# Mamba block with a top-2 mixture of LoRA experts on one core: new orders of the side jobs between the scans

## The chip, the cores and the metric

The kernel runs on one core of a Trainium2 chip. The metric is the device time of one launch in microseconds (us); of several runs the median counts.

## What is computed

The input is `u` with 4 sequences of 2048 tokens of 256 numbers. The block is pre-norm, with two residual branches:

```
x = u + mamba(layernorm(u));  out = x + moe(layernorm(x))
mamba:  x, z = split(u @ W_in.T + b_in)                       # 512 and 512 columns
        dt, B, C = split(x @ W_x.T + b_x)                     # 16, 16, 16
        delta = softplus(dt @ W_dt.T + b_dt);  A = -exp(A_log)
        h[t] = h[t-1] * exp(delta[t] * A) + x[t] * delta[t] * B[t]     # 512 x 16 states
        y[t] = sum over states of h[t] * C[t];  y = (y + x * D) * silu(z);  return y @ W_out.T + b_out
moe:    w = softmax(x @ Wg.T + bg), kept for the best 2 of 4 experts
        h_e = relu(x @ Wi.T + (x @ A_e.T) @ B_e.T);  return sum_e w_e * (h_e @ Wo.T)
```

All of it is in fp32. The recurrence over time is the part that no engine but VectorE does here, as a scan instruction.

## The kernel before

The 4 x 2048 tokens are cut into 16 chunks of 512 tokens, one after the other (the four sequences take turns). With 16 states for each of 512 channels, a chunk has 64 scans of 128 partitions x 512 tokens. They are grouped into 16 steps `s` of four scans `j`; four steps share a block `m` of 128 channels. The program below is each engine's own list of instructions, with semaphores between the lists. No scheduler moves anything: each engine works strictly through its list.

For each step there is a fixed skeleton:

- ScalarE (ACT) makes `decay = exp(delta * A)` for each scan into four PSUM banks (L1203), and keeps the last state of each scan (L1217, `keep_state`): after scans 0 and 1 have been multiplied by C, and after scans 2 and 3. The first two decays of a step can be made only after the keep for scans 0 and 1 of the step before.
- GpSimd (POOL) makes the scans' inputs `dx * B` for the next step (L1470, `times_b`), and in twelve of the 16 steps multiplies the last two scans by C (L1482, `times_c`).
- VectorE (DVE) does the four scans (L1395) and the other products with C (L1382).
- TensorE (PE) sums over the states into `y_ps` (L998, `sum_states`), two steps behind the scans. The sums of a block may start only when DVE has read the block before (`gated`, L1287).

All other work of the block is cut into small side jobs. A job is a letter and a number, and the same name stands in the tables of each engine that has a part in it. `pre` jobs belong to the next chunk, `main` to this one, `post` to the chunk before and `late` to the one before that. The jobs that the text speaks of, with their lines on PE and ACT or DVE:

- O: normalise the input (ACT L1159 on `xin`), for which GpSimd makes the last factor (L692). A: transpose it (PE L908). B, E: products with W_in (PE L914; B read by ACT at L1066, E at L1126). C, D: products that give B, C and delta (PE L918, L921; ACT L1101 is the last reader of a D).
- V, W, Z: after E, three more ACT steps for the sigmoid (L1129, L1132, L1135). S `main`: DVE multiplies it into `silu` (L1282), which frees E's bank. Y `main`: DVE makes `gated` (L1287).
- F: product with W_out and the residual (PE L933 to L940, ACT L1071). P, R, Q: second layer norm (ACT L1080, L1147 to L1153, L1159 on `xr`). G: transpose its result (PE L908 on `xr`, copied by ACT L1163). H0: the router's product (PE L946), read by DVE at L1325; H1 to H9, M0, M1: DVE's choice of the two experts.
- J, S: the two halves of the experts' hidden layer (PE L962 to L966 and L885; ACT L1177, L1181). T: transpose them (PE L979; ACT copy L1186). K: product with Wo (PE L984), added by DVE at L1298.
- L, M: ACT's exp and log for the softplus (L1108, L1113); V and U on GpSimd: the DMA that adds to it (L1460) and the product `delta * x` (L1450).

The order of the jobs is written out in tables, one row for each step. A row of PE has two parts (before and after `sum_states`), a row of ACT or DVE four, one behind each scan or decay:

```python
for job in side("act", c, s, j, parts):
    job_act(*job, c, par)
```

`SIDE` holds for chunks 0 to 14 (with small changes `FIRST` and `SECOND` for the start), `LAST` for chunk 15, `END` for what remains after the last scan. Products go to three PSUM banks. `assign_banks` runs through PE's table and gives each job the bank that, by the tables, is free first, so a new order also gives new banks, and with them new waits of PE for the engine that reads a bank.

Of the kernel before, what the change touches and what calls it, by code (L numbers as in the profile page):

```python
# [54 lines left out]
    "F1 post, F2 post, A1 pre | E0 main, F3 post, B0 pre",
    " | T3 late",
    "J4 late, B1 pre | B2 pre, B3 pre, S4 late",
    "E1 main | ",
    "J5 late, C0 pre | ",
    "C1 pre, K1 late, D0 pre | S5 late",  # L60
# [2 lines left out]
    "J6 late, J7 late, S6 late | ",
    "K2 late, S7 late | T6 late, E3 main",
    "T7 late, I0 post | K3 late",
    "J0 post, D2 pre | D3 pre, S0 post, J1 post",
    "J2 post, S1 post | T0 post",
# [1491 lines left out]
```

## Time and profile before

| | us |
|---|---|
| three runs | 1881.43, 1888.95, 1902.90 |
| median of the three | 1888.95 |
| the profiled execution | 1869.98 |
| its span, first to last instruction | 1868.2 |
| busy: DVE / GpSimd / PE / ACT | 1765.0 / 1717.0 / 1641.5 / 1505.7 |
| mean granted TensorE clock, share of full | 0.95 |

The profiled execution is 1.0% faster than the median of the others, which differ by 1.1% among themselves. Stage times below are of the profiled execution and count from the start of its span. Chunk 0's first scan starts at 39.8, chunk 8's at 910.5, chunk 15's at 1674.7, and the last scan ends at 1786.1.

### The profile page before, as it was taken

The numbers are of one execution on the slowest core, as the hardware profiler recorded it, in microseconds if no ns is written. First come the engines' busy times: TensorE is split into PE (matmuls) and PEld (weight loads), VectorE is DVE, ScalarE is ACT, GpSimd is POOL, SyncE is SP. The second block draws the span as 40 slices with busy tenths as digits, with TensorE's granted clock in tenths as the row PEclk, the third lists the DMA queues.
The fourth block names the chain that finished last, engine by engine and source line by source line (L and its number), as shares of the span: only waits on it lengthen the run. The fifth ranks groups of instructions, "written<-read, shape, count | busy, mean of one in ns | idle before, by whom it ended". The sixth has DMA issues, their size and how long they took to land.

```text
span 1868.2 us, 26288 instructions
## 1 busy us (share of the span) xinstructions
PE 1641.5 (88%) x7052; PEld 834.3 (45%) x7052; DVE 1765.0 (94%) x2060; ACT 1505.7 (81%) x3113; POOL 1717.0 (92%) x649
## 2 busy tenths in 40 slices
PE   6646689998998999899899989989998998998999
PEld 3213244444444444444444444444444544444465
DVE  5999999999999999999999999999999999999941
ACT  4776789788888978888897888889788898977743
POOL 1999999999999999999999999999999999999810
PEclk9767889999999999999999999999999999999999
DMA  6565566656647565654756565575656657565100
GB/s 209 137 142 142 109 153 141 163 119 143 151 99 172 132 170 120 148 142 104 174 129 168 126 144 143 105 173 132 163 128 142 144 105 175 120 160 133 42 18 17
DMA packets 150070, 249.07 MB, mean 133 GB/s; under 512 B 22432, under 2 KB 47264, under 8 KB 149408
## 3 DMA queue, kind: packets, MB, share of 16 engines
q1 hardware_dynamic: 145456, 231.09, 51.2%
q0 software_dynamic: 4464, 16.25, 4.5%
q8 instruction: 61, 1.00, 0.2%
q14 instruction: 89, 0.73, 0.1%
HBM read 188.01 MB, written 42.99 MB: 124 GB/s over the span
## 4 chain that ended last, share of the span: by engine, by line
PE 38%; DVE 30%; issue 13%; ACT 8%; POOL 5%; DMA 2%; SPq 1%; DVEq 0%; ACTq 0%; POOLq 0%
DVE decay L1395 13%; DVE hs L1382 8%; PE bank L914 7%; DVE hs L1395 5%; PE y_ps L998 5%; PE bank L962 5%; PE bank L984 4%; PE bank L936 4%; POOL hs L1470 3%; PE bank L918 3%; ACT decay L1203 2%; POOL hs L1482 2%; PE y_ps L1002 2%; PE bank L908 1%; PE bank L979 1%
## 5 line engine op out<-in xcount | busy, mean ns | idle before, releaser
L1470 POOL TENSOR_TENSOR hs<-dx_rep,b_rep 128x2048 f32<-128x2048 f32 x255 | 1180.6, 4643 | 43.6 <-DVE hs L1411 39.7
L1395 DVE TENSOR_TENSOR_SCAN decay<-decay,state,hs 128x512 f32<-128x512 f32 x640 | 798.7, 1288 | 6.3 <-ACT decay L1203 5.2
L1203 ACT ACTIVATE decay<-dt_rep,a_sb 128x512 f32<-128x512 f32 x1024 | 696.2, 686 | 20.6 <-DVE dx_rep L1409 1.8
L1395 DVE TENSOR_TENSOR_SCAN hs<-decay,state,hs 128x512 f32<-128x512 f32 x384 | 491.5, 1280 | 3.9 <-ACT decay L1203 3.8
L1482 POOL TENSOR_TENSOR hs<-hs,c_rep 128x1024 f32<-128x1024 f32 x192 | 469.3, 2444 | 5.3 <-ACT state L1217 4.6
L1382 DVE TENSOR_TENSOR hs<-decay,c_rep 128x1024 f32<-128x1024 f32 x320 | 389.0, 1216 | 0.0
L998 PE MATMUL y_ps<-hs,nsum 128*32 128x512 f32 x2048 | 291.6, 643 | 61.4 <-POOL hs L1482 40.4
L962 PE MATMUL bank<-w_i_sb,x_t 128*128 128x512 f32 x488 | 259.9, 658 | 5.4 <-DVE silu L1282 5.1
L914 PE MATMUL bank<-xn_t,w_in_sb 128*128 128x512 f32 x512 | 249.8, 616 | 12.2 <-DVE silu L1282 4.3
L984 PE MATMUL bank<-w_o_sb,r_t 128*128 128x256 f32 x944 | 221.0, 388 | 10.3 <-ACT r L1181 6.2
L984 PEld LDWEIGHTS bank<-w_o_sb,r_t 128*128 128x128 f32 x944 | 177.6, 192 | 65.0 <-ACT r L1181 18.2
L1217 ACT COPY state<-decay 128x2 f32<-128x2 f32 x320 | 50.4, 157 | 159.8 <-DVE hs L1382 156.7
L914 PEld LDWEIGHTS bank<-xn_t,w_in_sb 128*128 128x128 f32 x512 | 91.7, 194 | 125.7 <-issue 98.3
L979 PE MATMUL bank<-ident,r 128*128 128x128 f32 x928 | 121.7, 277 | 17.2 <-DVE x L1298 14.3
L962 PEld LDWEIGHTS bank<-w_i_sb,x_t 128*128 128x128 f32 x488 | 89.1, 200 | 104.3 <-issue 86.3
L979 PEld LDWEIGHTS bank<-ident,r 128*128 128x128 f32 x928 | 101.8, 140 | 75.6 <-issue 42.7
L998 PEld LDWEIGHTS y_ps<-hs,nsum 128*32 128x32 f32 x2048 | 41.8, 110 | 172.5 <-issue 150.0
L936 PE MATMUL bank<-w_out_sb,gated 128*128 128x256 f32 x480 | 114.0, 380 | 0.1
L1181 ACT ACTIVATE r<-bank,wgt 128x512 f32<-128x512 f32 x122 | 82.3, 675 | 33.0 <-PE bank L885 33.0
L936 PEld LDWEIGHTS bank<-w_out_sb,gated 128*128 128x128 f32 x480 | 91.6, 191 | 13.2 <-DVE gated L1287 0.5
L885 PE MATMUL bank<-lora_st,low_t 64*128 64x512 f32 x122 | 61.0, 500 | 41.1 <-ACT r L1177 40.8
L1177 ACT ACTIVATE r<-bank,wgt 128x512 f32<-128x512 f32 x122 | 82.8, 678 | 15.5 <-PE bank L966 12.2
(182 smaller groups left out, 1853.8 us busy)
## 6 DMA issues: line engine op xcount, KB each, us to landing
dx_rep<-rep_scratch SPq DMA_DIRECT2D x252, 256.0 KB, 4.7
dt_rep<-rep_scratch SPq DMA_DIRECT2D x252, 256.0 KB, 7.6
b_rep<-bc_scratch SPq DMA_DIRECT2D x256, 64.0 KB, 4.0
c_rep<-bc_scratch SPq DMA_DIRECT2D x256, 64.0 KB, 2.4
rep_scratch<-z_dt SPq DMA_DIRECT2D x64, 256.0 KB, 2.6
rep_scratch<-e_dt SPq DMA_DIRECT2D x64, 256.0 KB, 2.8
e_dt<-z_dt POOLq DMA_DIRECT2D x31, 512.0 KB, 4.9
xin<-in_u SPq DMA_DIRECT2D x16, 512.0 KB, 4.0
```

The source lines that it names most:

```text
L914: mm = pe.matmul(ps[:], w_in_sb[:, k, col:col + P], xn_t[odd][:, k, :], start=k == 0, stop=k == KD - 1)
L936: pe.matmul(ps[:, cols], gated[odd][:, k, i * P:(i + 1) * P], w_out_sb[:, k, :], start=k == 0 and is_last(q) and i % 2 == 0, stop=False, s ...
L962: pe.matmul(ps[:], x2_t[odd][:, k, t * P:(t + 1) * P], w_i_sb[:, k, cols], start=k == 0, stop=False, skip_group_check=is_last(q))
L979: mm = pe.matmul(ps[:, f * P:(f + 1) * P], r[i % 2][:, f * P:(f + 1) * P], ident[:], start=r is r1, stop=r is r2, is_transpose=True)
L984: mm = pe.matmul(ps[:, 0:D], r_t[:, f, :], w_o_sb[:, f, :], start=f == 0, stop=f == NF - 1)
L998: mm = pe.matmul(y_ps[32 * j:32 * j + 32, :], nsum[:], hs[s % 4][:, j, :], start=k == 0, stop=k == KG - 1, skip_group_check=True)
L1177: nc.scalar.activation(r1[i % 2][:], ps[:], ACT.Relu, scale=wgt[odd][:, 0, i // 2:i // 2 + 1]).then_inc(r1_ready, 1)
L1203: nc.scalar.activation(decay[:, j, :], dt_rep[m % 2][:, j, :], ACT.Exp, scale=a_sb[:, J * s + j:J * s + j + 1]).then_inc(decay_ready, 1)
L1382: v.tensor_tensor(hs[s % 4][:, js, :], decay[:, js, :], c_rep[:, k, :].unsqueeze(1).to_broadcast([P, 2, T]), ALU.mult).then_inc(prod_vecto ...
L1395: v.tensor_tensor_scan(hs[s % 4][:, j, :] if kept else decay[:, j, :], decay[:, j, :], hs[s % 4][:, j, :], state[:, b, n:n + 1], ALU.mult, ...
L1470: nc.gpsimd.tensor_tensor(hs[s % 4][:], dx_rep[m % 2][:], b_rep[:, k, :].unsqueeze(1).to_broadcast([P, J, T]), ALU.mult).then_inc(input_re ...
L1482: nc.gpsimd.tensor_tensor(hs[s % 4][:, 2:4, :], hs[s % 4][:, 2:4, :], c_rep[:, k, :].unsqueeze(1).to_broadcast([P, 2, T]), ALU.mult).then_ ...
```

## The change

Only the tables change: the same jobs, each exactly once in its table as before, stand in other rows, parts or orders. No instruction is added or removed, and the skeleton of decays, scans, products with C and sums stays as it is. GpSimd's tables keep their order within a chunk. The banks follow from PE's new tables.

```diff
 PE_SIDE = [
-    "K0 late | S3 late, T2 late",
-    " | A0 pre, F0 post",
+    " | K0 late",
+    "T2 late | F0 post, S3 late, A0 pre",
...
-    "T4 late, E2 main | T5 late, D1 pre, G0 post, G1 post",
-    " | H0 post",
+    "K1 late, D0 pre | S5 late, T4 late, E2 main, D1 pre",
+    " | T5 late",
+    "G0 post, G1 post | H0 post, J6 late",
...
 ACT_SIDE = [
-    " |  | R1 pre | S2 late, J3 late, O0 pre, O1 pre",
+    "S2 late |  | R1 pre, J3 late | T2 late, O0 pre",
...
-    " | F2 post, E0 main | V0 main, W0 main, Z0 main | ",
+    " | A1 pre, E0 main, V0 main | F2 post, W0 main | Z0 main, F3 post",
...
-    "C0 pre | C1 pre, J5 late |  | Q0 post, D0 pre",
+    "C0 pre | C1 pre, J5 late | Q0 post, Q1 post | D0 pre",
...
 DVE_SIDE = [
-    " |  | K0 late, Y3 post | ",
+    " | Y3 post | K0 late | ",
...
 DVE_LAST = [
-    "S0 main |  |  | K0 late",
+    " | K0 late | S0 main | ",
```

The lists below are of chunk 2, which has the same tables as the chunks up to 14. First ACT in step 4, before: the last decay of step 3, then those of step 4.

```order
L1203 ACTIVATE decay<-dt_rep,a_sb 128x512
L1071 ACTIVATE x_1,sum<-bank 128x256
L1060 COPY xn_t<-bank 128x512
L1217 COPY state<-decay 128x2
L1203 ACTIVATE decay<-dt_rep,a_sb 128x512 x2
L1071 ACTIVATE x_1,sum<-bank 128x256
L1126 ACTIVATE e_gate<-bank,high_z 128x512
L1217 COPY state<-decay 128x2
L1203 ACTIVATE decay<-dt_rep,a_sb 128x512
L1129 ACTIVATE e_gate<-e_gate,bound 128x512
L1132 ACTIVATE e_gate<-e_gate 128x512
L1135 ACTIVATE e_gate<-e_gate 128x512
```

And the same place now:

```order
L1217 COPY state<-decay 128x2
L1203 ACTIVATE decay<-dt_rep,a_sb 128x512 x2
L1060 COPY xn_t<-bank 128x512
L1126 ACTIVATE e_gate<-bank,high_z 128x512
L1129 ACTIVATE e_gate<-e_gate,bound 128x512
L1217 COPY state<-decay 128x2
L1203 ACTIVATE decay<-dt_rep,a_sb 128x512
L1071 ACTIVATE x_1,sum<-bank 128x256
L1132 ACTIVATE e_gate<-e_gate 128x512
L1203 ACTIVATE decay<-dt_rep,a_sb 128x512
L1135 ACTIVATE e_gate<-e_gate 128x512
```

A1's copy (L1060) and the first sigmoid step (L1129) now stand ahead of the third decay of step 4, and the last sigmoid step (L1135) behind the fourth.

PE ahead of the router's product, before, from the sums of step 6 on:

```order
L998 MATMUL y_ps<-hs,nsum 32x512 x4
L885 MATMUL bank<-lora_st,low_t 128x512
L979 MATMUL bank<-ident,r_0 128x128 x8
L914 MATMUL bank<-xn_t,w_in_sb 128x512 x2
L998 MATMUL y_ps<-hs,nsum 32x512 x4
L979 MATMUL bank<-ident,r_1 128x128 x8
L921 MATMUL bank<-dt_st,w_dt_st 128x512
L908 MATMUL bank<-ident,xr 128x128 x8
L998 MATMUL y_ps<-hs,nsum 32x512 x4
L946 MATMUL bank<-w_ga_sb,x_t 128x20 x8
```

And now:

```order
L998 MATMUL y_ps<-hs,nsum 32x512 x4
L885 MATMUL bank<-lora_st,low_t 128x512
L979 MATMUL bank<-ident,r_0 128x128 x8
L914 MATMUL bank<-xn_t,w_in_sb 128x512 x2
L921 MATMUL bank<-dt_st,w_dt_st 128x512
L998 MATMUL y_ps<-hs,nsum 32x512 x4
L979 MATMUL bank<-ident,r_1 128x128 x8
L908 MATMUL bank<-ident,xr 128x128 x8
L998 MATMUL y_ps<-hs,nsum 32x512 x4
L946 MATMUL bank<-w_ga_sb,x_t 128x20 x8
```

D1 (L921) moved from just ahead of the transposes G0 and G1 (L908) to the far side of the sums of step 7. By the new banks G0 goes where D1 was, and G1 where T5 (the second L979) was.

## Rows read from the trace of the kernel before

**Rows 1.** The page's first part: busy time, share of the span, instructions.

```profile
PE 1641.5 (88%) x7052; PEld 834.3 (45%) x7052; DVE 1765.0 (94%) x2060; ACT 1505.7 (81%) x3113; POOL 1717.0 (92%) x649
```

**Rows 2.** Windows by stage: length, busy time (count) of each engine, PE clock, DMA share, GB/s.

```profile
core 0: us, PE busy (x) PEld busy (x) DVE busy (x) ACT busy (x) POOL busy (x), PEclk, DMA share, GB/s
...
363.70:1674.70 1311.00, 1201.27 (x5245) 616.05 (x5244) 1301.62 (x1502) 1126.47 (x2341) 1295.73 (x493) 0.98 0.60 140
910.50:1019.10 108.60, 99.28 (x438) 51.09 (x437) 108.39 (x126) 93.80 (x196) 107.39 (x42) 0.98 0.61 143
1019.10:1128.70 109.60, 100.51 (x438) 51.48 (x437) 108.48 (x126) 93.73 (x196) 108.71 (x43) 0.97 0.59 140
1674.70:1786.10 111.40, 102.06 (x453) 54.34 (x452) 108.31 (x119) 82.42 (x172) 98.94 (x34) 0.95 0.38 87
1786.10:1868.20 82.10, 77.58 (x332) 51.12 (x332) 17.41 (x54) 28.01 (x53) 0.20 (x1) 0.98 0.04 12
```

**Rows 3.** Waits of DVE: us in total, times, longest.

```profile
DVE lg L1325 <- PE bank L946: 6.0, 8, 0.9
DVE decay L1395 <- ACT decay L1203: 5.2, 8, 1.4
...
DVE hs L1395 <- ACT decay L1203: 3.8, 15, 0.5
...
DVE decay L1395 <- issue: 0.8, 1, 0.8
```

**Rows 4.** Waits of GpSimd.

```profile
POOL z_dt L1450 <- DMA e_dt<-z_dt: 4.4, 10, 0.9
```

**Rows 5.** Timeline of chunk 9, router's product: start, us, instruction, idle before.

```profile
1085.83 0.65 PE L908 MATMUL bank<-ident,xr 128*128 128x128 f32 x4 [1.54 <-ACT e_dt L1101]
...
1088.20 1.94 PE L998 MATMUL y_ps<-hs,nsum 128*32 128x512 f32 x8
...
1092.17 0.17 DVE L1325 TENSOR_TENSOR lg<-bank,b_g_sb 128x16 f32<-128x16 f32 x1 [0.76 <-PE bank L946]
```

**Rows 6.** Window over those sums of chunk 9 (columns as in rows 2).

```profile
1086.90:1090.30 3.40, 3.14 (x13) 1.15 (x14) 3.40 (x4) 3.37 (x8) 3.40 (x1) 0.50 1.05 208
```

**Rows 7.** The same place in chunk 8.

```profile
978.97 1.06 PE L998 MATMUL y_ps<-hs,nsum 128*32 128x512 f32 x8
...
982.56 0.17 DVE L1325 TENSOR_TENSOR lg<-bank,b_g_sb 128x16 f32<-128x16 f32 x1
```

**Rows 8.** Timeline of chunk 8, step 4: the gate's chain on ACT, and DVE.

```profile
939.12 0.69 ACT L1126 ACTIVATE e_gate<-bank,high_z 128x512 f32<-128x512 f32 x1 [0.82 <-PE bank L914]
...
940.09 0.69 ACT L1203 ACTIVATE decay<-dt_rep,a_sb 128x512 f32<-128x512 f32 x1
940.72 0.71 ACT L1129 ACTIVATE e_gate<-e_gate,bound 128x512 f32<-128x512 f32 x1
...
940.93 1.30 DVE L1395 TENSOR_TENSOR_SCAN hs<-decay,state,hs 128x512 f32<-128x512 f32 x1
...
942.12 0.63 ACT L1135 ACTIVATE e_gate<-e_gate 128x512 f32<-128x512 f32 x1
...
943.22 0.79 DVE L1282 SCALAR_TENSOR_TENSOR silu<-bank,b_in_sb,e_gate 128x512 f32<-128x512 f32 x1
```

**Rows 9.** Timelines of ACT and of DVE in chunk 1, around its second step.

```profile
159.60 1.09 ACT L1159 ACTIVATE xin<-xin,nt,rs 128x256 f32<-128x256 f32 x2 [3.65 <-POOL nt L692]
...
161.56 1.29 DVE L1395 TENSOR_TENSOR_SCAN decay<-decay,state,hs 128x512 f32<-128x512 f32 x1 [1.42 <-ACT decay L1203]
```

**Rows 10.** Timeline of DVE in chunk 15: K0, and the start of step 13.

```profile
1695.85 0.42 DVE L1298 TENSOR_TENSOR x<-bank,x 128x256 f32<-128x256 f32 x1 [0.83 <-PE bank L984]
...
1766.73 2.47 DVE L1395 TENSOR_TENSOR_SCAN decay<-decay,state,hs 128x512 f32<-128x512 f32 x2 [1.14 <-ACT decay L1203]
```

**Rows 11.** Timelines of DVE and of PE after the last scan.

```profile
1792.40 0.69 DVE L1287 TENSOR_TENSOR gated<-y_ps,silu 128x512 f32<-128x512 f32 x1 [5.04 <-PE y_ps L998]
...
1861.81 3.69 PE L984 MATMUL decay<-w_o_sb,r_t 128*128 128x256 f32 x16 [0.87 <-ACT r_t L1186]
```

More of the change, by code:

```diff
@@ L51 @@
 PE_SIDE = [
-    "T1 late | S2 late, J3 late",
-    "K0 late | S3 late, T2 late",
-    " | A0 pre, F0 post",
[L55 to L60, printed above, removed]
-    "T4 late, E2 main | T5 late, D1 pre, G0 post, G1 post",
-    " | H0 post",
[L63 to L67, printed above, removed]
[16 rows of a table added]
 ]
 ACT_SIDE = [
[16 rows of a table removed]
[16 rows of a table added]
 ]
@@ L134 @@
     "",
-    "",
     "K0 late",
@@ L139 @@
     "K1 late",
+    "",
     "",
@@ L145 @@
     "",
+    "K3 late",
     "",
-    "K3 late",
 ]
@@ L152 @@
     "T1 late | J3 late",
-    " | E0 main",
-    "S2 late, F0 post | ",
-    "K0 late, E1 main | S3 late, F1 post, F2 post, F3 post",
-    " | T2 late",
-    "T3 late | J4 late, K1 late, S4 late",
-    " | T4 late",
-    "J5 late | S5 late",
-    "G0 post | E2 main",
-    " | T5 late, G1 post",
-    "J6 late, H0 post, S6 late | K2 late, J7 late",
-    " | S7 late, T6 late, T7 late",
-    "K3 late, I0 post | J0 post, E3 main",
-    "S0 post, J1 post | S1 post",
-    "T0 post, T1 post | ",
-    "J2 post, K0 post, S2 post | ",
[15 rows of a table added]
 ]
 ACT_LAST = [
[16 rows of a table removed]
[16 rows of a table added]
 ]
@@ L193 @@
     " | Y3 post |  | ",
[1 row of a table removed]
+    " |  |  | ",
+    " | K0 late | S0 main | ",
     " |  |  | ",
     " |  |  | ",
[2 rows of a table removed]
+    " |  | K1 late, Y0 main | ",
     " |  |  | ",
[5 rows of a table removed]
+    "S1 main |  |  | ",
+    " |  |  | H0 post, Y1 main",
+    "S2 main, H1 post | H2 post, K2 late, H3 post | H4 post | H5 post",
+    "H6 post | H7 post, H8 post | H9 post | M0 post",
+    "K3 late, M1 post |  |  | ",
     " | Y2 main |  | ",
[2 rows of a table removed]
+    " |  | K0 post | ",
+    " | S3 main |  | ",
 ]
@@ L237 @@
     "",
-    "",
     "K1 late",
@@ L241 @@
     "",
-    "K2 late",
-    "K3 late, K0 post",
+    "K2 late, K3 late",
     "",
@@ L247 @@
     "",
+    "",
+    "K0 post",
 ]
 PE_END = [
[16 rows of a table removed]
[16 rows of a table added]
 ]
 ACT_END = [
[16 rows of a table removed]
[16 rows of a table added]
 ]
 DVE_END = [
[16 rows of a table removed]
+    "Y3 post |  |  | ",
+    "F0 post |  |  | ",
+    "F1 post | F2 post |  | F3 post",
+    "P0 post, P1 post | O2 post | H0 post, H1 post | H2 post",
+    "H3 post |  | H4 post | ",
+    "H5 post, H6 post |  | H7 post | ",
+    "H8 post |  |  | ",
+    " | M0 post |  | M1 post, H9 post",
+    "K1 late | R0 post |  | ",
+    " | R1 post, K2 late |  | ",
+    "R2 post |  | R3 post | ",
+    "K3 late |  |  | ",
+    "K0 post |  |  | K1 post",
+    " |  |  | R4 post, R5 post",
+    "R6 post, R7 post | K2 post |  | ",
+    " | K3 post |  | ",
 ]
 POOL_END = [
+    "",
+    "",
+    "",
     "",
@@ L324 @@
     "",
+]
+SP_END = [
+    "",
+    "K1 late",
     "",
@@ L327 @@
     "",
-]
-SP_END = [
-    "K1 late",
-    "",
-    "",
-    "K2 late",
+    "K2 late",
+    "",
     "K3 late",
+    "K0 post, K1 post",
     "",
@@ L341 @@
     "",
-    "K0 post, K1 post",
-    "",
-    "",
     "",
     "K2 post, K3 post",
-    "",
 ]
```

177 rows, old and new, of tables (ACT_END, ACT_LAST, ACT_SIDE, DVE_END) are left out of this document.

## The prediction

> **What bounds the kernel now.** I read the busy shares first. DVE leads with 1765.0 us of a span of 1868.2, GpSimd follows with 1717.0 [rows 1]. A share over the whole span mixes start, steady chunks and tail, so the windows by stage come next [rows 2]. Twelve steady chunks take 1311.0 us, 109.25 each, and DVE is busy for 1301.6 of them, 99.3%. GpSimd is at 98.8%, PE at 92%, ACT at 86%. The reader should see that all of one chunk's DVE work, some 108.4 us, is fixed: the change removes no instruction. Single chunks come in two lengths, 108.6 (chunk 8) and 109.6 (chunk 9), with DVE's work the same to 0.1 us. After the last scan the picture turns: in the last 82.1 us PE is busy for 77.6 and DVE for 17.4.
>
> So an order can only win what DVE waits for between its scans, and what PE waits for in the tail. DVE's list of waits gives the first: 6.0 us for the router's product, 5.2 + 3.8 for decays, 0.8 with no releaser [rows 3] and 0.8 for one K [rows 10], together **16.6 us, or 0.9% of the time**. The tail holds 82.1 - 77.6 = 4.5 us more, part of which is the last add and store.
>
> The base: the profiled execution took 1869.98, the median of the three runs is 1888.95, a factor of 1.0101. The runs differ by 1.1%, so about 1% is what a measurement of this kernel can tell from no change. I make the sum on 1870.0 and multiply.
>
> **The change part by part.**
>
> *Start of chunks 0 and 1.* In chunk 1 ACT waits 3.65 us for GpSimd's factor, then does O0 and O1 (1.09 for two) before it may keep a state and make the next decay, for which DVE waits 1.42 [rows 9]. Now only O0 stands there. One O, 1.09 / 2 = 0.5, goes off the path in each of the two chunks: **-1.0**. Bounds: 0 (the log-exponential job L1 now follows in chunk 0's gap and takes it back) to -2.7, all of both waits. I take the row's own half.
>
> *The router's place, chunks 3 to 14.* Where do chunk 8 and chunk 9 part? In both, PE waits 1.54 before G0, since G0 goes into D1's bank, which ACT still reads (shown for chunk 9, [rows 5]). In chunk 9 the sums that follow take 1.94 for eight matmuls, in chunk 8 1.06 [rows 5, 7], and the granted clock over them is 0.50, the lower level, 1.2 GHz [rows 6]. The router's product behind them ends late, and DVE waits 0.76 for it; in chunk 8 it doesn't wait [rows 7]. That is the 6.0 us in 8 waits [rows 3], 0.75 each, and the whole difference between the chunk lengths. Now D1 stands ahead of the sums of step 7, so the 1.54 before G0 goes. But G1 takes T5's bank, and ACT copies T5 only behind the second decay of step 10, ahead of G0's copy: PE will wait about as long, one transpose later, for T5's copy instead. ACT's copy of G1 comes one T copy later (T5's, about 0.6) and 0.4 earlier, because Q1 now fills a wait in step 8: +0.2. The clock may thus fall at this place as often as before. I take **0**. Bounds: -6.0 if PE never slows there, and if it does in every one of 12 chunks, 12 x (0.76 + 0.2) - 6.0 = +5.5.
>
> *Step 4 and the gate, chunks 1 to 14.* Before, ACT waits 0.82 for E0's product, reads it from 939.12 to 939.81, and the third decay is ready at 940.78 for a scan that starts at 940.93; Z0 ends at 942.75, silu starts at 943.22 [rows 8]. Now V0 (0.71) stands ahead of that decay, and Z0 behind the fourth. If E0 came when it did before, V0 would push the end of the decay from 940.78 to 941.49; DVE's scan, due at 940.93, would be about 0.5 late, and Z0 another 0.2: 0.7 a chunk. But PE should reach E0 earlier: T2 no longer waits for DVE to read K0's bank, as its new bank is J2's, and F3 and B0 were behind E0 before and are now too. Walking PE's list from T2 on with these durations I get E0 about 1.0 earlier, and then ACT is at E0 just before it is needed. What hides V0 is thus that 1 us. I take **0**, with slack of no more than 0.1 or 0.2 at silu; bounds 0 to +9.1 (13 chunks, 2 to 14, of 0.7), and more if PE is slow (the first rival).
>
> *K0, Y3, Y0, K2, K3 and M1 on DVE; the sums on PE.* These cost DVE the same in any place. Y3 moves ahead of K0 and frees the sums of the next block sooner; Y0 moves 2 scans later. The sums of step 4 wait for it, and behind them on PE stands C0; GpSimd's input for step 8 needs those sums, but it comes behind its input for step 7 and product of step 5, some 3 us later. 0. In steps 13 and 14 D2 goes to K3's bank: PE waits until DVE has added K3, and ACT's D2 and J0 stand ahead of the fourth decay of step 14. By the walk this decay is ready just in time. 0, bounds 0 to +0.2 a chunk.
>
> *GpSimd.* Its list is unchanged; it waited 4.4 us for the softplus sum's DMA, 10 times [rows 4]. M1, which that DMA waits for, stands one part later, behind F1 and a decay, some 1.2 us; no wait for M1 is in GpSimd's list before, so I take 0, bounds 0 to +1.2 a chunk less the slack that GpSimd has on DVE. On SP's queue only the stores of K3 and the like shift a step; nobody waits for them.
>
> *Chunk 15.* DVE came to K0 0.83 before its product was there, and waited 1.14 for a decay at step 13 that stood behind J0 and S0 on ACT [rows 10]. K0 is now two scans later, so 0.8 goes. The routing steps H4 to M1 come one to four scans earlier, so J0 and S0 are ready sooner: 1.1 goes. **-1.9**, bounds -3.1 (all waits of the chunk: 111.4 - 108.3 [rows 2]) to +3, if the new places make waits of the same size.
>
> *Tail.* PE is full, and its jobs are the same, so its 77.6 us stay. Y0 and Y1 now run ahead of the last sums in place of J5, which brings these about a microsecond forward, and with them the gated product that DVE waited 5.04 for [rows 11]. What can go is a wait like the 0.87 before the last K [rows 11]. **-1.0**, bounds -4 to +6: the order there is wholly new, and a job whose input isn't ready stops all behind it.
>
> Sum: -1.0 + 0 + 0 - 1.9 - 1.0 = **-3.9**, 1866.1 us profiled, times 1.0101 = **1885.0**. DVE's floor doesn't move, and most of its waits were small or come back.
>
> **The rivals.**
>
> *Slower: E0 comes late (15%).* Mechanism: V0 and A1's copy stand ahead of a decay that DVE needs, behind a product that PE must deliver. Price: 0.7 a chunk if PE is as late as before, and each microsecond more of PE adds one. If PE's new waits (for DVE's K0 ahead of F0, for O3 ahead of A0) drop its clock there, the four matmuls of E0 and those ahead of it double. At 1.0 later than before it is 1.7 x 13 = 22.1 us: 1870.0 + 22.1 - 3.9 = 1888.2, times 1.0101 = **1907.3**. It decides from about 1.0 later than before; below 0.7 earlier it costs nothing. For it: ACT did wait 0.82 for E0 [rows 8]. Against it: T2's freed wait, and a clock that reads 0.98 over the steady chunks [rows 2].
>
> *Faster: all waits vanish (12%).* The router's 6.0 go, both starts' 2.7, chunk 15's 3.1, the 3.8 for the decays of `hs`, and 2 in the tail: about -17.6, 1852.4, times 1.0101 = **1871.1**. For it: the 1.54 wait and the low clock stand side by side. Against it: the decay in step 8 (0.2 in 15 chunks, most of the 3.8) keeps its C1 and J5 ahead of it.
>
> *The clock falls more often (15%).* What the rows show: a lower clock right behind PE's waits of 1.54, in a PE that is 92% busy. The new order cuts one such wait and makes others in steps 1, 2 and 10. If each chunk slows at the router: +5.5 - 3.9 = +1.6, 1871.6 profiled, **1890.5**. The Trainium skill ("TensorE: Matmul & The Clock Gate", section "A second HAM failure mode: psum-queue depth-cycling") says that a PE that idles shortly and often while it cycles through PSUM banks can swing between its two clocks; by that rule a new spread of short waits over three banks may swing as much as the old one. The trace agrees as far as 0.50 over the sums of chunk 9 goes [rows 6].
>
> *A worse tail (8%).* If one ACT or DVE job sits in front of another that PE needs, PE idles; +6 gives 1870.0 - 2.9 + 6 = 1873.1, **1892.1**.
>
> **How the numbers follow.** Forecast 50%, the rivals 15, 12, 15 and 8. Predicted is the forecast, 1885. Its terms' bounds and the third and fourth rival lie between 1872 and 1895; the range takes in the fast case, 1871, and the slow one in part, as the sums with the spread of the runs have it: 1868 to 1904. Over 1% slower is above 1907.8: a little over half of the first rival, and parts of the last two and of the forecast where two bad bounds meet the spread of the runs, 15%. Over 1% faster is below 1870: the fast case is just short of it, and with the spread of the runs I give 12%. The rest, 73%, is within 1%.
>
> **What would show it.** In the profile after, steady chunks of 108.6 to 109.6; DVE's wait for L946 between 0 and 12 us; no idle before silu (L1282) or the third scan of step 4 above 0.2; in chunks 0 and 1 a wait of about 0.9 for the first decay of step 2; chunk 15 near 109.5; a tail near 81. Wrong would be a steady DVE share below 98%, or a tail above 86.

## The result and the profile after

The changed kernel takes 1855.74 us (median of 4 runs, 1854.72 to 1856.80), the kernel before 1885.19 (4 runs, 1878.01 to 1902.90); the ratio is 0.988, with an interval of 0.984 to 0.992. The forecast was 1885.0, and its range began at 1868: the result lies below both. Runs over 1.5% above the fastest of their kernel are left out of the ratios, medians and ranges below. Two things differ from the forecast at once. The profiled execution went from 1869.98 to 1855.82, 14.2 us less where 3.9 were summed. And the changed kernel's runs lie within 2.1 us of each other and of the profiled one, while those of the kernel before reach up to 1.8% above theirs.

The page's first part of the changed kernel: DVE's busy time is the same to 1.3 us [rows 1], so nearly all of the 14 are waits.

```profile
PE 1624.7 (88%) x7052; PEld 830.2 (45%) x7052; DVE 1763.7 (95%) x2060; ACT 1503.9 (81%) x3113; POOL 1714.5 (92%) x649
```

Windows by stage of the changed kernel: the twelve steady chunks, chunks 8 and 9, chunk 15, the tail (columns as in rows 2).

```profile
362.30:1665.30 1303.00, 1185.29 (x5253) 612.72 (x5252) 1300.97 (x1502) 1124.80 (x2341) 1293.98 (x494) 0.99 0.59 141
906.30:1014.70 108.40, 99.05 (x438) 51.25 (x437) 108.39 (x126) 93.78 (x196) 107.88 (x42) 0.98 0.60 142
1014.70:1123.10 108.40, 98.77 (x446) 51.59 (x445) 108.39 (x126) 93.76 (x196) 107.77 (x42) 1.00 0.59 142
1665.30:1775.20 109.90, 100.76 (x450) 53.51 (x449) 108.05 (x119) 82.10 (x172) 99.44 (x34) 0.97 0.38 88
1775.20:1854.00 78.80, 74.36 (x327) 49.51 (x327) 17.47 (x55) 27.99 (x53) 0.20 (x1) 1.00 0.04 12
```

Beside [rows 2]: steady chunks 1311.0 to 1303.0, ten of them now of 108.4, with DVE busy for 99.8%. The other two are chunk 12 with 108.6 and chunk 6 with 110.3: chunks 3 to 10 run as a loop of four chunks, taken twice, and at its turn, behind chunk 6, DVE waits 1.84 (0.84 before). Further: chunk 15 111.4 to 109.9; the tail 82.1 to 78.8; chunks 0 to 2 lose 1.7 between them and the first scan comes 0.3 later. That makes the 14.2: 8.0 + 1.5 + 3.3 + 1.7 - 0.3.

DVE's list of waits in the changed kernel, against [rows 3]. The wait for a decay with `hs` came 15 times and comes once, and of the eight for the router's product (seven of 0.69 to 0.91 in steady chunks, one of 0.21 in chunk 15) the one in chunk 15 is left, now 0.77; the other of the two here, of 10.1, is in the tail.

```profile
DVE lg L1325 <- PE bank L946: 10.9, 2, 10.1
...
DVE decay L1395 <- ACT decay L1203: 3.9, 4, 1.8
...
DVE hs L1395 <- ACT decay L1203: 0.8, 1, 0.8
```

The router's place. First one row of the kernel before that the prediction left out, PE's timeline in chunk 9, right behind the wait of 1.54 in [rows 5]: the second transpose, G1, waits once more, for ACT's copy of G0 out of the same bank.

```profile
1087.16 1.11 PE L908 MATMUL bank<-ident,xr 128*128 128x128 f32 x4 [0.68 <-ACT x_t L1163]
```

PE's timeline of the changed kernel at the same place, chunk 8:

```profile
970.79 1.09 PE L979 MATMUL bank<-ident,r 128*128 128x128 f32 x8
972.21 0.63 PE L908 MATMUL bank<-ident,xr 128*128 128x128 f32 x4 [0.32 <-ACT xr L1159]
974.01 0.66 PE L908 MATMUL bank<-ident,xr 128*128 128x128 f32 x4 [1.18 <-ACT r_t L1186]
974.60 1.06 PE L998 MATMUL y_ps<-hs,nsum 128*32 128x512 f32 x8
975.83 1.96 PE L946 MATMUL bank<-w_ga_sb,x_t 128*128 128x20 f32 x16 [0.16 <-ACT x_t L1163]
```

DVE's read of the product there, without a wait, and the window over the place with its granted clock of 1.00:

```profile
978.15 0.16 DVE L1325 TENSOR_TENSOR lg<-bank,b_g_sb 128x16 f32<-128x16 f32 x1
```

```profile
972.00:978.00 6.00, 4.45 (x33) 3.08 (x34) 6.00 (x6) 5.87 (x13) 6.00 (x3) 1.00 1.06 223
```

G0 and G1 now have banks of their own. PE's waits ahead of the router's product were 1.54 + 0.68, and another 0.29 at H0 in some chunks; they are 0.32 + 1.18, and 0.16 to 0.25 at H0. The sums of step 8 take 1.06 or 1.07 in every chunk, as they did in [rows 7] and not in [rows 5]. The lower clock, found at this place in 7 of the 12 steady chunks before, now lies near it in one, chunk 12, where DVE doesn't wait.

### The profile page after: what moved, and what is told of

Read it like the earlier page. It is cut to its first block, busy times and chain, and to the rows that moved or that the text cites. A ratio compares the mean times of both kernels' runs of the same rounds, so it can differ in the third digit from the quotient of the medians.

```text
span 1854.0 us, 26281 instructions
## 1 busy us (share of the span) xinstructions
PE 1624.7 (88%) x7052; PEld 830.2 (45%) x7052; DVE 1763.7 (95%) x2060; ACT 1503.9 (81%) x3113; POOL 1714.5 (92%) x649
## 4 chain that ended last, share of the span: by engine, by line
DVE 35%; PE 18%; issue 17%; POOL 16%; ACT 7%; DMA 2%; SPq 1%; DVEq 0%; POOLq 0%; ACTq 0%
DVE decay L1395 15%; POOL hs L1470 10%; DVE hs L1382 9%; DVE hs L1395 7%; POOL hs L1482 4%; PE bank L914 3%; PE bank L962 3%; ACT decay L1203 3%; PE y_ps L998 2%; PE bank L984 2%; POOL z_dt L1450 2%; PE bank L918 1%; DMA b_rep<-bc_scratch 1%; DVE silu L1282 1%; PE bank L979 1%
## 5 line engine op out<-in xcount | busy, mean ns | idle before, releaser
L1395 DVE TENSOR_TENSOR_SCAN hs<-decay,state,hs 128x512 f32<-128x512 f32 x384 | 485.8, 1265 | 1.3 <-ACT decay L1203 0.8
L1482 POOL TENSOR_TENSOR hs<-hs,c_rep 128x1024 f32<-128x1024 f32 x192 | 476.5, 2482 | 6.0 <-ACT state L1217 5.8
L1382 DVE TENSOR_TENSOR hs<-decay,c_rep 128x1024 f32<-128x1024 f32 x320 | 383.7, 1199 | 0.0
L962 PE MATMUL bank<-w_i_sb,x_t 128*128 128x512 f32 x492 | 249.6, 631 | 8.2 <-DVE silu L1282 6.9
L984 PE MATMUL bank<-w_o_sb,r_t 128*128 128x256 f32 x944 | 217.0, 383 | 4.7 <-ACT r_t L1186 2.7
L979 PE MATMUL bank<-ident,r 128*128 128x128 f32 x920 | 120.8, 278 | 6.4 <-ACT r L1181 4.3
L979 PEld LDWEIGHTS bank<-ident,r 128*128 128x128 f32 x920 | 100.6, 141 | 52.2 <-DVE x L1298 15.6
L936 PE MATMUL bank<-w_out_sb,gated 128*128 128x256 f32 x496 | 118.0, 380 | 0.3 <-DVE gated L1287 0.3
L1186 ACT COPY r_t<-bank 128x512 f32<-128x512 f32 x119 | 69.4, 583 | 17.8 <-PE bank L979 13.4
```

The costliest lines, as they stand in the source:

```text
L936: pe.matmul(ps[:, cols], gated[odd][:, k, i * P:(i + 1) * P], w_out_sb[:, k, :], start=k == 0 and is_last(q) and i % 2 == 0, stop=False, s ...
L962: pe.matmul(ps[:], x2_t[odd][:, k, t * P:(t + 1) * P], w_i_sb[:, k, cols], start=k == 0, stop=False, skip_group_check=is_last(q))
L979: mm = pe.matmul(ps[:, f * P:(f + 1) * P], r[i % 2][:, f * P:(f + 1) * P], ident[:], start=r is r1, stop=r is r2, is_transpose=True)
L984: mm = pe.matmul(ps[:, 0:D], r_t[:, f, :], w_o_sb[:, f, :], start=f == 0, stop=f == NF - 1)
L1382: v.tensor_tensor(hs[s % 4][:, js, :], decay[:, js, :], c_rep[:, k, :].unsqueeze(1).to_broadcast([P, 2, T]), ALU.mult).then_inc(prod_vecto ...
L1395: v.tensor_tensor_scan(hs[s % 4][:, j, :] if kept else decay[:, j, :], decay[:, j, :], hs[s % 4][:, j, :], state[:, b, n:n + 1], ALU.mult, ...
```

## The experiments

Times are of the profiled execution's span unless called medians. "At the router" means 66 to 69 us behind a chunk's first scan, and counts are of the 12 steady chunks, 3 to 14. Where a kernel has its banks written out, its lines are numbered 3 higher than in the kernel before (L946 is L949), in the one with added work up to 9 higher.

**Which tables carry the gain?** Two kernels, one with the new `SIDE` and `LAST`, one with the new `LAST` and `END`.

In the first, all `SIDE` and `LAST` tables are those of the changed kernel and the `END` tables those of the kernel before.

> The new tables for chunks 0 to 15, the old ones for what comes after the last scan. If the gain of the change lies in the chunks (steady chunks 108.4 instead of 109.25, chunk 15 at 109.9 instead of 111.4), this keeps about 11 us of the 14.2 us of the profiled executions: span 1857, tail 82. If the tail's order carries more, the tail stays above 82 and the span above 1860. In the timed runs it should be as narrow as the changed kernel (within 0.2%) if the scatter of the kernel before comes from its chunks.

Measured: span 1858.7, median 1859.41 (1857.05 to 1860.86, 4 runs), ratio 0.989 [0.984, 0.994]. Steady chunks of 108.4, chunk 15 109.9, tail 82.0.

In the second, `LAST` and `END` are those of the changed kernel and `SIDE` is as before.

> The old tables for chunks 0 to 14, the new ones for chunk 15 and the tail. If the tail and chunk 15 carry 4.8 us (3.3 + 1.5), span 1863 to 1864 with steady chunks still alternating between 108.6 and 109.6, and DVE still waits for the router's product some 0.75 us in about half of the chunks. The timed runs should scatter as the kernel before does (1878 to 1903) if the scatter sits in chunks 0 to 14.

Measured: span 1863.8, median 1870.68 (1865.69 to 1884.41, 8 runs), ratio 0.996 [0.993, 0.9995]. Chunks of 108.6 and 109.6 as before, chunk 15 109.9, tail 78.9. So the tail is 3.2 to 3.3 shorter with `END`, and chunk 15 is 1.5 shorter with `LAST`, in these two surroundings; `SIDE` is worth the rest, and only with it do the runs agree with each other. The sizes of the first two don't hold everywhere: with the old `LAST` and `END` but the router's rows (below), chunk 15 takes 110.3 and the tail 80.4.

**Is it D1's place?** The kernel before, with D1 moved as in the change.

```diff
-    "T4 late, E2 main | T5 late, D1 pre, G0 post, G1 post",
+    "T4 late, E2 main, D1 pre | T5 late, G0 post, G1 post",
...
-    "S5 late | Q1 post | Q2 post, T4 late | Q3 post, D1 pre",
+    "S5 late | Q1 post | Q2 post, T4 late | D1 pre, Q3 post",
```

> The kernel before with one job moved: D1 ahead of the sums of step 7 on PE, and ahead of Q3 on ACT (banks follow). Theory 1 (PE's long wait ahead of G0 lowers its clock over the router's product, and DVE waits for that): DVE's waits for L946 in the chunks go from 6.0 us to 0 or nearly, steady chunks 108.6, span 1862. Theory 2 (the steady gain comes from the many other moves): no change, 1868 with the same waits of 0.75.

Measured: span 1938.1, median 1939.09, ratio 1.032 [1.026, 1.037]. Chunks 2 to 14 take 112.8 to 117.6: the simple theory missed by over 70 us. In chunk 8 the timelines of PE, ACT and DVE show why:

```profile
1024.26 3.52 PE L962 MATMUL bank<-w_i_sb,x_t 128*128 128x512 f32 x4 [2.52 <-DVE silu L1282]
...
1028.25 0.69 ACT L1177 ACTIVATE r<-bank,wgt 128x512 f32<-128x512 f32 x1 [5.87 <-PE bank L966]
...
1029.55 1.29 DVE L1395 TENSOR_TENSOR_SCAN decay<-decay,state,hs 128x512 f32<-128x512 f32 x1 [3.81 <-ACT decay L1203]
```

The move gave J6 the bank of E2 instead of T5's. E2 is read last by DVE's `silu`, so PE waits 2.52; PE's J6 then runs at the lower clock (3.52 for four matmuls that take 1.96 elsewhere); ACT waits 5.87 to read it, and behind that read in ACT's list stands a decay that DVE needs: 3.81 in this chunk, 56 in the 13 chunks from 2 to 14.

The same move again, but with the banks written out so that J6 still follows T5 (F1, F2, J7, T7 and I0 get their old neighbours back too, while J0 and D2 change places):

```diff
-            bank[name] = free.index(min(free))
+            bank[name] = KEPT[name]
```

> The kernel before with D1 moved as in the changed kernel, as in the run before that came out at 1939, but with J6, J7 and the jobs up to K3 written into the banks that keep their old neighbours: J6 waits for T5's read again, not for E2's. Theory A (bank order): the 57 us that D1's move alone cost were J6 waiting 2.5 for DVE's silu through E2's bank and ACT's read of J6 standing ahead of a decay. Then DVE's waits of 3.8 a chunk are gone and the profiled span is 1866 to 1872. What is left open is the router: G0 now follows Q3's read on ACT instead of D1's, PE still waits about 1.3 there, so the lower clock and the waits for the router's product should stay: about 6 us of them, and the timed runs should scatter over 10 us or more. Theory B (D1's place is itself bad): span above 1890.

Measured: span 1875.9, median 1874.49 (1867.05 to 1882.28), ratio 0.994 [0.990, 0.998]. 62 us of the 70 came from the banks, most of them from J6's. PE waits 1.26 + 0.68 ahead of the router's product, the lower clock is there in 5 chunks, DVE waits 7.0 for the product. The router's waits stay, as expected; the span missed its range (1866 to 1872) by one long chunk 2 of 113.5. The median is 0.6% below that of the kernel before, a gain that the interval holds and the profile at hand doesn't show.

**Is it DVE's wait itself?** DVE's first routing step one scan later, so that it doesn't meet the late product.

```diff
-    " |  | H0 post | H1 post, S2 main, H2 post",
-    "H3 post | H4 post | H5 post | H6 post",
+    " |  |  | H0 post, S2 main, H1 post",
+    "H2 post, H3 post | H4 post | H5 post | H6 post",
```

> The kernel before, only DVE's routing steps H0 to H2 one place later, behind the last scan of step 10. PE's waits and clock stay as they are. Theory 1: the low clock still comes behind the 1.54 us wait, but DVE comes 1.3 us later to the router's product and no longer waits: steady chunks 108.6, span about 1862. If DVE's time is lost to the low clock in another way, the chunks keep alternating and the span stays at 1868. If the scatter of the timed runs of the kernel before is this wait too, they come down to 1865; if not, they stay at 1878 to 1903.

Measured: span 1872.4, median 1881.10 (8 runs), ratio 1.002 [0.997, 1.006]. The waits for L946 are gone from the steady chunks, and nothing is won: the lower clock is now at the router in all 12 chunks, and DVE waits for a decay behind it instead, 0.3 to 0.4 in each. Its waits for decays come to 12.5 against 5.2 [rows 3], of which 2.8 are at the loop's turn (0.8 before, with no releaser).

**Where do the 0.2 in step 8 come from?** C0's product one step earlier on PE.

```diff
-    "E1 main | ",
-    "J5 late, C0 pre | ",
+    "E1 main | C0 pre",
+    "J5 late | ",
```

The banks are written out as they were.

> The kernel before with C0's product one step earlier on PE, as in the changed kernel, all banks as before. In chunk 8 ACT starts to read C0 0.74 after the decay ahead of it, 0.62 in the changed kernel, and J5's and C1's reads follow. Theory A: the 0.21 that DVE waits in every chunk for the third decay of step 8 hangs on that; it goes in all 15 chunks, -3 us, and the long chunks with the lower clock at the router stay: steady chunks of 108.4 and 109.4, span 1865, median within 0.4% of before's. Theory B (the wait hangs on DVE's own slower scans of step 7 and 8, or on the order of Q1): the 0.2 stays, span 1868.

Measured: span 1874.9, median 1889.78 (1876.21 to 1902.38), ratio 1.002 [0.998, 1.007]. The wait in step 8 is gone in all but two chunks. But the lower clock stands at the router in all 12, every chunk is 109.2 or longer, and DVE's waits for the product add up to 12.0. In this profile the small saving ahead of the router went with a worse router; the runs as a whole can't be told from those of the kernel before.

**The router's rows, alone and put back.** PE's and ACT's steps 8 to 11 of the change put into the kernel before (with K2 moved out of PE's step 12), and the reverse, with banks written out to match:

```diff
-    "C1 pre, K1 late, D0 pre | S5 late",
-    "T4 late, E2 main | T5 late, D1 pre, G0 post, G1 post",
-    " | H0 post",
...
+    "C1 pre, K1 late, D0 pre | S5 late, T4 late, E2 main, D1 pre",
+    " | T5 late",
+    "G0 post, G1 post | H0 post, J6 late",
...
-    "S5 late | Q1 post | Q2 post, T4 late | Q3 post, D1 pre",
-    "G0 post |  | G1 post, E2 main | T5 late, V2 main, W2 main, Z2 main",
...
+    "Q2 post |  | S5 late | T4 late, D1 pre, Q3 post",
+    " | T5 late, G0 post | G1 post | E2 main, V2 main, W2 main, Z2 main",
```

> The kernel before with the whole neighbourhood of the router on PE and ACT (steps 8 to 11) as in the changed kernel, banks forced to the changed kernel's neighbours there; the rest of the chunk, chunk 15 and the tail are as before. Theory A (the low clock at the router comes from PE's wait of 1.5 ahead of G0, which these rows take away): no wait of DVE for the router's product, steady chunks of 108.4 to 108.7, span 1859 to 1862, timed runs within 4 us of each other. Theory B (the clock there is set by what PE does in the rest of the chunk): the lower clock stays at the router in half the chunks, span 1866 to 1870, runs scattered over 15 us.

Measured: span 1867.3, median 1869.01 (1868.27 to 1872.13, 4 runs), ratio 0.990 [0.983, 0.997]. No wait for the router's product in any steady chunk, and runs within 4 us, as theory A had it. But the span is 5 above theory A: the lower clock has gone to another place, 14 us into seven of the chunks.

> The changed kernel with the same four rows put back on PE and ACT, banks forced to the old neighbours. Theory A: PE waits 1.5 for D1's reader ahead of G0 again, chunks of 108.4 and 109.4 alternate, DVE waits about 6 us for the router's product, span 1860 to 1862, timed runs scattered over 10 us or more with the lowest at 1861. Theory B: chunks stay at 108.4, span 1855, median 1856.

Measured: span 1865.0, median 1874.92 (1864.50 to 1882.70, 10 runs), ratio to before 0.993 [0.989, 0.997]. Ten of the 12 chunks have the lower clock at the router and take 109.2 (the one with the loop's turn 110.9), two take 108.4. Chunk 9: the whole chunk, the 3.4 us at the router, and PE's rows there.

```profile
1020.90:1130.10 109.20, 99.21 (x439) 50.97 (x437) 108.52 (x127) 93.74 (x196) 108.23 (x42) 0.98 0.60 141
1088.30:1091.70 3.40, 3.15 (x14) 1.16 (x14) 3.40 (x4) 3.37 (x8) 3.40 (x1) 0.51 1.06 210
```

```profile
1087.21 0.66 PE L911 MATMUL bank<-ident,xr 128*128 128x128 f32 x4 [1.48 <-ACT e_dt L1104]
1088.55 1.11 PE L911 MATMUL bank<-ident,xr 128*128 128x128 f32 x4 [0.68 <-ACT x_t L1166]
1089.59 1.94 PE L1001 MATMUL y_ps<-hs,nsum 128*32 128x512 f32 x8
```

These two are the strongest pair: the same rows remove and restore the lower clock at the router and the waits for the product. The scatter of the runs goes and comes back with them too (4 us over 4 runs, 18 over 10).

**Is it PE's wait that brings the lower clock?** The kernel before with work added and no order changed: 12 needless matmuls in the wait ahead of G0.

```diff
...
+                if job[:2] == "D1" and twice:
+                    b5 = used("T5", c, AHEAD["late"])[0]
+                    for f in (0, 1, 0, 1, 2, 3):
+                        for r in (r1, r2):
+                            mm = pe.matmul(banks[b5][:, f * P:(f + 1) * P], r[1][:, f * P:(f + 1) * P], ident[:],
+                                           start=r is r1, stop=r is r2, is_transpose=True)
+                    mm.then_inc(filled[b5], 1)
```

> The kernel before, order and banks untouched, with needless work added: behind D1 and ahead of G0, where PE waits 1.54 for ACT's read of D1, PE transposes parts of r for T5's bank once more (12 matmuls, about 1.3 by T5's own 8 in 0.85), and T5 counts as filled only after that; ACT reads it 6 later. Nothing of the result changes. Theory A (PE's wait itself brings the lower clock on, and that makes the router's product late): the lower clock leaves the router's place, DVE's waits for the product go, all steady chunks are 108.6, the span is about 1862, and the timed runs lie within 5 us. Theory B (the place of the lower clock is set by the order of the work around, not by this wait): more work makes PE later, DVE waits for the router's product in more chunks than before, the span is 1870 to 1876 and the runs scatter as before.

Measured: median 1869.70 (1866.39 to 1876.18), ratio 0.996 [0.994, 0.998]; span 1870.0. PE's timeline in chunk 9:

```profile
1085.64 1.47 PE L992 MATMUL bank<-ident,r 128*128 128x128 f32 x12
1087.35 0.66 PE L908 MATMUL bank<-ident,xr 128*128 128x128 f32 x4 [0.23 <-ACT e_dt L1110]
1088.68 0.66 PE L908 MATMUL bank<-ident,xr 128*128 128x128 f32 x4 [0.68 <-ACT x_t L1172]
1089.26 1.07 PE L1007 MATMUL y_ps<-hs,nsum 128*32 128x512 f32 x8
```

The window over G0, G1 and these sums, clock 1.00:

```profile
1087.10:1090.50 3.40, 2.32 (x17) 0.99 (x16) 3.40 (x4) 3.34 (x9) 3.40 (x2) 1.00 1.06 216
```

With 1.47 us more work in a chunk the lower clock is gone from the router in all 12 (in two it lies 4 us later), and the kernel gets faster by 0.4%. That is theory A's mechanism. Its numbers were too good: the lower clock appears instead 14 us into ten of the chunks, at the same place as with the router's rows, chunk 15 is 1.4 longer, and the ten runs still scatter over 10 us where 5 were expected.

**How much do the router, C0 and the ends explain together?** The router's rows, C0 early, and `LAST` and `END` of the change; steps 0 to 7 and 12 to 15 otherwise as before.

```diff
-    "E1 main | ",
+    "E1 main | C0 pre",
...
```

> The kernel before with only these parts of the change: PE's and ACT's steps 8 to 11, C0 one step earlier on PE, and the tables for chunk 15 and the tail. Not in it: the new rows of steps 0 to 7 and 12 to 15 on PE, ACT and DVE. Theory A (the router's rows, C0 and the tail are the whole gain): steady chunks of 108.4, chunk 15 109.9, tail 78.8, span 1855 to 1858, median within 0.2% of the changed kernel's 1855.7. Theory B (the other rows carry part of it): DVE waits of 0.2 to 0.5 remain in steady chunks as in the run with the router's rows alone, span 1860 or more.

Measured: span 1861.1, median 1865.88 (1862.92 to 1871.23), ratio 0.993 [0.990, 0.996]. Theory B is right here. Chunks take 108.7 to 109.4 (chunk 6, with the loop's turn in it, 111.2), except two of 108.4 in which the clock never falls. Windows over chunk 9, the stretch 14 us into it, and chunk 14; then PE there:

```profile
1018.80:1127.80 109.00, 100.67 (x438) 51.77 (x437) 108.62 (x127) 93.48 (x196) 108.02 (x42) 0.97 0.59 142
1032.90:1036.30 3.40, 3.40 (x17) 1.41 (x16) 3.40 (x4) 3.35 (x7) 3.40 (x2) 0.50 0.37 68
1564.00:1672.40 108.40, 97.96 (x438) 50.82 (x437) 108.38 (x127) 93.74 (x196) 107.91 (x42) 1.00 0.58 137
```

```profile
1030.92 0.49 PE L888 MATMUL bank<-lora_st,low_t 64*128 64x512 f32 x1 [0.61 <-ACT r L1180]
1032.54 1.67 PE L982 MATMUL bank<-ident,r 128*128 128x128 f32 x8 [1.13 <-DVE x L1301]
1034.14 1.94 PE L1001 MATMUL y_ps<-hs,nsum 128*32 128x512 f32 x8
```

T2 (L982) waits 1.13 for DVE to read K0 out of its bank: the wait that the change takes away by giving T2 the bank of J2. (In chunk 14 T2 waits 1.06, and the clock stays up.) Behind the sums PE is then 1.5 later than in chunk 14, and 43 us on DVE waits 0.2 to 0.3 for the third decay of step 8 in most of these chunks.

**T2's wait.** First the changed kernel with steps 0 to 5 put back (0 to 6 on DVE; D2 and D3 change banks), then the kernel just shown with nothing but banks changed, T2 into J2's (A0 then follows K0, and J0 and D2 change places).

```diff
-    " | K0 late",
-    "T2 late | F0 post, S3 late, A0 pre",
...
+    "K0 late | S3 late, T2 late",
+    " | A0 pre, F0 post",
...
```

> The changed kernel with the rows of steps 0 to 5 (PE, ACT), 0 to 6 (DVE) and SP's to match put back as they were, so that T2 again goes into K0's bank and PE waits for DVE there; banks forced so that only this part has the old neighbours. Theory A (the wait at T2 is where the lower clock goes once the router is clean, and it makes a later decay late): the lower clock at 13.6 to 14.5 into the chunk as in the run with router, C0 and ends, chunks of 108.8, DVE idle 0.3 in them, span 1860 to 1862, median 1863 to 1867. Theory B (the rows of steps 12 to 15 carry the rest of the gain): chunks of 108.4, median 1856.

```diff
-KEPT = {'T1': 0, 'J3': 1, 'K0': 0, 'T2': 0, 'A0': 2, 'F0': 0, ...
+KEPT = {'T1': 0, 'J3': 1, 'K0': 0, 'T2': 2, 'A0': 0, 'F0': 2, ...
```

> The kernel with router rows, C0 and ends, and no instruction moved against it: only the banks of T2 to D1 change hands, so that T2 goes where J2 was (read long before) and not where K0 was, and A0 goes to K0's. PE's wait of 1.13 ahead of T2 goes. Theory A (that wait brings the lower clock on): no lower clock at 14, chunks of 108.4, span 1857, median 1857 to 1860. Theory B (A0 waits in its place and PE stands as long, one job later): the lower clock stays at 14 to 18, chunks of 108.8, median 1866.

> The changed kernel again, on the chip of the two runs above, to compare them with: 1855.7 and runs within 2 us if its narrow spread isn't an accident of one chip; a spread of 10 us or more if it is.

The rows put back give 1870.6, median 1869.68 (1866.63 to 1872.52, 4 runs), some 9 above theory A. The lower clock is at 14.5 in 8 chunks as expected, and in these chunks DVE waits 0.8; but even without it DVE waits 0.50 for the first decay of step 7, because PE brings S4 late and ACT waits 0.91 for it ahead of that decay. T2's bank alone gives 1866.6, median 1864.87 (1863.98 to 1868.46, 4 runs): neither theory. Nine chunks are at 108.4 to 108.7 (109.9 with the loop's turn), and three take 111:

```profile
1019.20:1130.20 111.00, 102.17 (x447) 52.86 (x440) 108.91 (x126) 93.73 (x197) 107.94 (x43) 0.97 0.59 138
1037.70:1041.10 3.40, 3.40 (x9) 2.68 (x9) 3.40 (x4) 2.11 (x5) 3.40 (x2) 0.51 0.02 5
```

```profile
1033.69 1.06 PE L1001 MATMUL y_ps<-hs,nsum 128*32 128x512 f32 x8 [0.80 <-DVE gated L1290]
1035.41 0.66 PE L911 MATMUL bank<-ident,xin 128*128 128x128 f32 x4 [0.66 <-ACT xin L1162]
1037.42 0.91 PE L936 MATMUL bank<-xr,ident 128*128 128x256 f32 x2 [1.36 <-ACT r_t L1189]
1038.12 3.40 PE L939 MATMUL bank<-w_out_sb,gated 128*128 128x256 f32 x8
```

PE does T2 early and then waits three times for DVE and ACT; where the clock falls now, it falls on F0 (L939), and DVE waits 1.9 for decays in that chunk, the first 0.9 some 5 us later. Chunk 15 and the tail are longer in both runs than in the changed kernel, 110.8 and 111.0 against 109.9 and 80.5 against 78.8, although their tables are the same. The bank and the new row order of steps 0 to 5 belong together. The changed kernel once more, on the chip of these two: span 1854.3, median 1855.42 (1854.72 to 1856.65), ratio 0.985 [0.979, 0.990]. Its narrow spread holds.

**What is the scatter of the kernel before?** Two more profiles of it, unchanged.

> The kernel before once more, unchanged, for a second profile: its timed runs go from 1871 to 1903, while the profile at hand is of 1870. If the scatter is the router's place, a slower execution shows more or longer stretches of the lower clock there, with waits of DVE for the router's product or for a decay behind it of several us in single chunks, and everything else (DVE's work, tail) as in the first profile. The rival: the extra time is spread evenly, DVE's own instructions or the DMAs are slower.

> The same as the run before it, a third profile of the unchanged kernel, with the same two readings.

Measured: 1878.62 and 1879.89, spans 1876.8 and 1878.1. The lower clock is at the router in 9 chunks of each (7 in the first profile). In chunk 7 it lasts three times as long in both, and that chunk takes 113.0 and 112.9 where the first profile has 108.6. Windows over chunk 7 of the second profile, over the stretch, and over chunk 10, where the clock doesn't fall at the router; then DVE in chunk 7:

```profile
805.10:918.20 113.10, 103.81 (x437) 53.81 (x437) 108.76 (x126) 93.59 (x196) 105.80 (x42) 0.94 0.57 135
873.60:883.80 10.20, 10.20 (x33) 5.51 (x32) 8.04 (x15) 6.01 (x12) 10.20 (x3) 0.50 0.57 110
...
1137.40:1246.10 108.70, 99.36 (x438) 51.10 (x437) 108.48 (x127) 93.81 (x196) 107.62 (x42) 0.98 0.59 142
```

```profile
879.87 0.17 DVE L1325 TENSOR_TENSOR lg<-bank,b_g_sb 128x16 f32<-128x16 f32 x1 [2.16 <-PE bank L946]
...
885.43 1.29 DVE L1395 TENSOR_TENSOR_SCAN decay<-decay,state,hs 128x512 f32<-128x512 f32 x1 [1.61 <-ACT decay L1203]
```

DVE's own work in the chunk is the same to 0.3. Against the first profile, DVE's waits at the router, with the decay behind it, are 6.0 longer in the second, of 8.6 us more in the span, and 4.6 longer in the third, of 9.9. The third also starts its first scan 3.0 later and waits 1.4 longer at the loop's turn. So the router is the largest part of the scatter up to 1880, and not all of it. No execution above 1880 was profiled; what the slowest ones lose isn't shown.

## Why the prediction was wrong, step by step

Of the 29.3 us between forecast and result, 10.4 are in the sum (1866.1 profiled against 1855.8 measured, 1855.7 median) and 18.9 in the factor put on it.

*The base.* "I make the sum on 1870.0 and multiply." That step took the scatter for a property of the measurement. It belongs to the kernel: over 8 to 10 runs, the kernels that keep the old router rows scatter over some 10 us or more (1866 to 1884 with new `LAST` and `END`; 1865 to 1883 with the rows put back); those with the new ones scatter over 2 to 8, most of them in 4 runs only. The factor itself came from three runs: later medians of 7 to 24 runs of the kernel before are 1878.6 to 1882.5. The changed kernel's median is its profiled time. This alone would have put the forecast at 1866.1.

*The router, taken at 0, measured -5.8 in the steady chunks.* (Of the eight waits that the prediction counted as 0.75 each, one was of 0.21 in chunk 15.) The failed step is "PE will wait about as long, one transpose later, for T5's copy instead". As a wait it came true: 1.18 + 0.32 for G1 and G0, about the 1.54 that I compared it with. What failed is the conclusion from it, that the clock falls "as often as before": I compared one wait with two. Before, G1 shared G0's bank and waited another 0.68. PE's waits ahead of the router's product, and the steady chunks with the lower clock there:

| kernel | G0 + G1 (us) | chunks of 12 |
|---|---|---|
| before, three profiles | 1.54 + 0.68 | 7, 9, 9 |
| before, new `LAST` and `END` | 1.54 + 0.68 | 6 |
| before, H0 later | 1.54 + 0.68 | 12 |
| before, C0 early | 1.54 + 0.68 | 12 |
| after, router put back | 1.48 + 0.68 | 10 |
| before, D1 moved, banks kept | 1.26 + 0.68 | 5 |
| after, two profiles | 0.32 + 1.18 | 0, and 1 four us later; 0 |
| after, old `END` | 0.32 + 1.18 | 0 |
| router, C0, ends; T2's bank; first rows back | 0.32 + 1.18 | 0, and 1 four us later; 0; 0 |
| before, router's rows | 0.33 + 1.18 | 0 |
| before, wait filled | 0.23 + 0.68 | 0, and 2 four us later |

That the wait ahead of G0 brings the lower clock on at this place is shown by the filled wait, where nothing else changed. The table doesn't tell whether it is the split of the waits or their sum: the counts are 6 to 12 where the two add up to 2.2, 5 at 1.94, and 0 at 1.5 and below, and no run has the same sum in another split. Why the clock falls in one chunk and not in the next with the same waits no row shows either, and it stays open. The Trainium skill ("TensorE: Matmul & The Clock Gate", section "A second HAM failure mode: psum-queue depth-cycling") tells of a PE that idles briefly and often between groups and swings between its clocks; I used it for the rival that the new spread of waits swings as much as the old. The swing is there in all these kernels, but at the router it went with the two waits.

*The decays of step 8, taken as kept, measured gone: -2.8 in the steady chunks, -0.6 in chunk 2.* That the decay "keeps its C1 and J5 ahead of it" was true and beside the point. ACT waited for C0's product ahead of them (0.43 in chunk 8), and the new order asks for it a step earlier. The run with C0 early shows it. The loop's turn takes 1.0 back; with 0.65 less of DVE's own work the steady chunks come to their -8.0 within 0.3.

*K0, T2 and the first steps, taken at 0.* By their rows alone this held: V0's and Z0's new places cost nothing. ACT reads E0 0.8 earlier in chunk 8 than in [rows 8], where the walk gave 1.0, the third decay of step 4 ends 0.2 before its scan, and `silu` doesn't wait. PE's wait for DVE's K0 moved from T2 to F0 (1.39 in chunk 8), and the clock doesn't fall there. The term missed their worth once the router is clean: with the old steps 0 to 7 and 12 to 15, span 1861.1 instead of 1854.0 and the lower clock at 14 us.

*Starts: -1.0 against -1.0.* Chunks 0 and 1 went from 105.2 and 109.3 to 104.9 and 108.7, 0.9 together; the first decay of step 2 is waited for by 0.81 and 0.93, as said, but in chunk 0 the wait two scans later grew from 0.50 to 0.84.

*GpSimd, 0.* This held. Its waits of 4.4 for the DMA [rows 4] are gone from its list, and DVE waits for it 0.7 in all.

*Chunk 15: -1.9 against -1.5.* K0's and step 13's waits [rows 10] are gone; the router's product is now waited for by 0.77 instead of 0.21, in its earlier place, and a new wait of 0.31 stands before a `silu`.

*Tail: -1.0 against -3.3.* `gated` comes 2.1 earlier, the wait shrinks from 5.04 [rows 11] to 2.95, and the 0.87 before the last K stayed. The mis-sized part is PE's own pace. From the router's product to the end both kernels have 212 matmuls and nearly the same waits (1.75 and 1.62), in 56.0 and 54.2 us. Windows over that stretch and over the 3.4 us behind the product, before; and the whole stretch after:

```profile
1813.90:1817.30 3.40, 3.40 (x7) 1.65 (x7) 2.79 (x19) 0.00 (x0) 0.00 (x0) 0.51 0.07 23
1812.20:1868.20 56.00, 51.66 (x212) 34.07 (x212) 11.54 (x36) 17.18 (x30) 0.20 (x1) 0.97 0.05 17
```

```profile
1799.80:1854.00 54.20, 50.03 (x212) 33.39 (x212) 11.58 (x36) 18.24 (x32) 0.20 (x1) 1.00 0.05 18
```

One stretch of the lower clock, 1.7 to 1.8 us, undiluted because PE is the bound. It doesn't belong to `END`: with the old tables it is missing in the runs with C0 early and with the router's rows (54.2, tail 80.4), and with the new ones it comes back in the two runs on T2's wait (55.9, tail 80.5). What sets it isn't shown. The other 1.5 are in the 26.1 and 24.6 before the product: PE has 5 matmuls fewer to do there, with the new `END` in every surrounding, and that is what the tables are worth by themselves. Which of its rows brings PE ahead by the last scan wasn't tried. "Its 77.6 us stay" was the wrong step: PE is busy there for 74.4.

*The ranks.* The rival "all waits vanish" (12%) came nearest, with 1852.4 profiled against 1855.8, though most of the starts' waits and half of chunk 15's stayed; times 1.0101 it too came out at 1871.1.

## What to carry to other kernels

When an engine with slack (here PE, 92% busy) sometimes runs at its lower clock, list all its waits side by side at that place, not only the longest, and look at several chunks and several executions; a wait can be removed, split by a bank of its own, or filled with needless work. Treat a spread of the runs as something that the change may take away. And when one job is moved in a list from which buffers are assigned, look at who follows whom in every buffer: new neighbours in the banks cost some 60 us, more than the change was worth.
